# A graph layer on one core: the two kinds of node-sum products regrouped among the five rounds of a period

## The reference

```python
h = jnp.maximum(_layernorm(x, axis=-1), 0.0)
msg = h[src] + edge_attr_64
agg = jax.ops.segment_sum(msg, dst, num_segments=6250)
out = x + (jax.nn.relu(agg @ W1 + b1) @ W2 + b2)      # W1: 64 x 128, W2: 128 x 64
```

## Time and profile before

| | |
|---|---|
| median of 3 runs | 521.0 us (520.02 to 521.77) |
| the profiled execution | 520.01 us, its span 518.3 us |
| PE matmul busy | 460.3 us, 89% of the span |
| DVE busy | 434.3 us, 84% |
| ACT busy | 380.4 us, 73% |
| POOL busy | 317.0 us, 61% |
| granted TensorE clock, mean | 0.988 of full |

### The profile page before, as it was taken

How to read it: one execution, slowest core, us unless ns; L and a number is a source line. 1 busy time by engine, 2 the same in 40 slices (tenths; PEclk the granted TensorE clock), 3 DMA queues, 4 the chain that set the end, 5 groups by cost and what they waited for, 6 DMA issues and landing times.

```text
span 518.3 us, 27579 instructions
## 1 busy us (share of the span) xinstructions
PE 460.3 (89%) x12541; PEld 406.6 (78%) x12541; DVE 434.3 (84%) x531; ACT 380.4 (73%) x481; POOL 317.0 (61%) x223
## 2 busy tenths in 40 slices
PE   1012799999999999999999999999999999999994
PEld 1002688898898889889888988988898888888883
DVE  4989977989988988998898899889889989969550
ACT  2846766877877887788787878878787877878720
POOL 4379999846576576658757666767765665225200
PEclk9999979999999999999999999999999999999997
DMA  9758058743653573465367347436735743651300
GB/s 197 192 143 253 25 141 200 208 119 114 190 168 98 157 207 113 119 193 147 94 181 205 100 131 196 131 104 187 198 86 143 204 123 106 186 170 51 90 3 10
DMA packets 139626, 73.65 MB, mean 142 GB/s; under 512 B 23644, under 2 KB 137550, under 8 KB 139382
## 3 DMA queue, kind: packets, MB, share of 16 engines
q1 hardware_dynamic: 136105, 65.30, 45.7%
q0 software_dynamic: 3168, 4.90, 3.6%
q10 hardware_dynamic: 234, 1.65, 0.9%
HBM read 66.98 MB, written 4.86 MB: 139 GB/s over the span
## 4 chain that ended last, share of the span: by engine, by line
PE 85%; POOL 6%; DMA 3%; ACT 2%; DVE 2%; issue 1%; SPq 0%; ACTq 0%; DVEq 0%; POOLq 0%
PE sum_ps L846 26%; PE sum_ps L868 21%; PE count_ps L833 17%; PE sum_ps L854 14%; POOL ell L511 3%; PE sum_ps L883 3%; PE sum_ps L890 3%; POOL g L491 2%; DMA comb_rows<-counts 1%; PE sum_ps L818 1%; DMA dst_sb<-in_dst 1%; DMA ell<-comb_rows,ell_idx 1%; ACT counts L345 1%; ACT counts L347 1%; POOL r_f L498 1%
## 5 line engine op out<-in xcount | busy, mean ns | idle before, releaser
L409 ACT CAST counts<-count_ps 128x882 bf16<-128x882 f32 (+2 forms) x369 | 327.1, 978 | 59.7 <-PE count_ps L833 58.6
L677 DVE TENSOR_TENSOR lo_hot<-iota_lo,codes 128x3328 bf16<-128x3328 bf16 (+3 forms) x123 | 228.9, 1861 | 43.1 <-PE count_ps L833 26.4
L511 POOL DMA_INDIRECT ell<-comb_rows,ell_idx x50 | 96.6, 1932 | 92.2 <-DVE ell_idx L649 58.8
L846 PE MATMUL sum_ps<-counts,h_parts 128*128 128x256 bf16 (+1 forms) x1225 | 146.1, 273 | 0.0
L846 PEld LDWEIGHTS sum_ps<-counts,h_parts 128*128 128x128 bf16 x1225 | 114.8, 99 | 18.5
L833 PE MATMUL count_ps<-hi_hot,lo_hot 64*128 64x49 bf16 x6256 | 110.5, 183 | 16.5 <-DVE hi_hot L677 14.8
L833 PEld LDWEIGHTS count_ps<-hi_hot,lo_hot 64*128 64x128 bf16 x6256 | 96.1, 94 | 36.9 <-DVE hi_hot L677 18.0
L491 POOL DMA_INDIRECT g<-in_dst,row_i x49 | 95.0, 1938 | 45.0 <-DVE e_hot L691 29.0
L868 PE MATMUL sum_ps<-e_hot,edges 128*64 128x24 f32 x3528 | 113.1, 217 | 0.5 <-issue 0.5
L868 PEld LDWEIGHTS sum_ps<-e_hot,edges 128*64 128x64 f32 x3528 | 107.9, 139 | 3.2 <-issue 0.6
L677 DVE TENSOR_TENSOR hi_hot<-iota_hi,codes 128x1300 bf16<-128x1300 bf16 (+3 forms) x123 | 105.2, 856 | 0.0
(11 more groups left out here) (107 smaller groups left out, 208.9 us busy)
## 6 DMA issues: line engine op xcount, KB each, us to landing
edges<-in_edge_attr SPq DMA_DIRECT2D x98, 576.0 KB, 5.2
h_rows<-h_sb SPq DMA_DIRECT2D x1, 1568.0 KB, 10.6
x_sb<-in_x SPq DMA_DIRECT2D x4, 384.0 KB, 10.4
out<-o_sb SPq DMA_DIRECT2D x24, 64.0 KB, 1.7
comb_rows<-counts ACTq DMA_DIRECT2D x1, 1443.8 KB
dst_rows<-in_dst SPq DMA_DIRECT2D x49, 18.0 KB
ell<-comb_rows,ell_idx POOLq DMA_INDIRECT x50, 4.0
g<-in_dst,row_i POOLq DMA_INDIRECT x49, 3.9
```

The source lines that it names most:

```text
L409: nc.scalar.copy(counts[j % 2][:, :, 0:2 * half].rearrange("p s (h i) -> p h s i", h=2)[:, :, :, first + a:first + b], count_ps[u % 3][:, ...
L511: nc.gpsimd.indirect_dma_start(out=ell[j % 2][0:rows, h, :, :].rearrange("p s w -> p (s w)"), out_offset=None, in_=comb_dram[:, :], in_off ...
L677: return nc.vector.tensor_tensor(out_ap.rearrange("p i (a t) -> p i a t", t=2), bc(table_ap.rearrange("p (o a t) -> p o a t", o=1, t=2), [ ...
L846: nc.tensor.matmul(sum_ps[m % 2][:, 0:cols], parts[:, s, 0:2 * F], counts[m % 2][:, s, 0:cols], start=(s == 0), stop=False, skip_group_che ...
```

## The change

Only the two tables that deal the node-sum products to the rounds are changed. Nothing else is moved on any other engine, no instruction is added or dropped, and none is made larger or smaller.

```diff
-                HIGH = [0, 20, 20, 40, 40, 49]
-                LOW = [0, 0, 5, 5, 17, 49]
+                HIGH = [0, 24, 24, 49, 49, 49]
+                LOW = [0, 0, 0, 0, 0, 49]
```

## The result

The changed kernel takes 532.37 us at the median of 6 runs (531.04 to 533.89), the kernel before 521.08 us (6 runs beside them, 518.56 to 521.77). The ratio is 1.0208, with a 95% interval from 1.0185 to 1.023: about 2% slower. The profiled execution took 531.46 us with a span of 529.9 us; the one before had 518.3 us, so 11.6 us are to be found.

The account below looks back on a forecast made before the run. PE was taken to bound the kernel, with ACT's copies just fitting rounds 3 and 4. 520.0 - 1.0 (start) + 11.3 (middle) - 0.4 (end) = 529.9, plus 1.0 for the median: 530.9 us; own range 528 to 533, whole range 526 to 537.

Parts of the forecast that it names:

- The seams: Between PE's product groups: a change of the array's split costs about 0.10 us; PE alone saves 0.12 us a period.
- The seam that stood in no row: Edge matmuls followed by counting: taken as 2.12 + 0.10 = 2.22 us, with ends 2.12 and 2.30.
- The stall: Last third of round 4's counting: PE waits 0.67 us for ACT's round 3 copy in every period.
- PE alone decides: Rival, 7%: ACT's last round 3 copy ends early enough, no stall comes; 517.1 us.
- partly absorbed: Rival, 4%: part of the stall goes, for instance by faster ACT copies beside fewer products; half gives 524 us.
- The sum of the middle: Fourth to last counting period: 21 x 0.55 = 11.5 us, less 0.2 in period 22, gives +11.3.
- the 0.2 us foreseen for period 22: Period 22: one product more ahead of round 4 fills part of the stall, 0.2 us less.
- The start: Second period: moved products fill PE's idle time for DVE's tables, clock may stay up; -1.0 us, ends -2.3 and 0.
- The clock rival: Rival, 9%: idle time beside edge products lowers the clock, 2.75 us a fall; every third period gives about 550 us.
- DVE: DVE's batches: no cost, spare time of over 1 us a period; its waits for PE up some 12 us.
- the shortest stretch of two rounds: Counting that DVE's batches need two rounds earlier: rounds 3 and 4 named as shortest, 7.47 us against 7.58.
- at most 0.4 us later: End of the edge products that SP's loads of edges wait for; costed at nothing, with four buffers.

Follow-up runs that it names:

- low_kept: Changed kernel with table LOW as in the kernel before (5, 12, 32) and only HIGH changed; 543.31 us, ratio 1.0232.
- twelve_back: Changed kernel with 12 of the 64-column products put back into round 3, HIGH as changed; 556.19 us, ratio 1.0387.
- short_copies: Changed kernel with ACT's three round 3 copies taking only the first tile of each pair in periods 2 to 23; 551.27 us, ratio 1.0421.
- before_here: The kernel before, unchanged, run again on the third chip; 522.05 us, ratio 0.9991.
- changed_here: The changed kernel as it is, run again on the third chip; 532.26 us, ratio 1.0191.
- turns_first: Changed kernel with PE's turns of round 2 ahead of that round's 25 products, from the fourth period on; 549.07 us, ratio 1.0346.
- six_back: Changed kernel with 6 of the 64-column products put back into round 3; 546.56 us, ratio 1.0302.

## Why the prediction was right, point by point

**The seams.** Right. Rounds 0 to 3 were forecast at 4.02, 3.58, 3.73 and 3.20 us and measured 4.02, 3.58, 3.72 and 3.20. The seam that stood in no row, edges followed by counting, cost 259.87 - 257.65 = 2.22 us, the 0.10 that I chose out of 0 to 0.18. Without the stall, `low_kept`, `twelve_back` and `short_copies` show 18.13, 18.14 and 18.11 us a period; the forecast for PE alone was 18.13.

**The stall.** Right in place, cause, number and size. I gave 0.67 us, 21 times, in the last third of round 4's counting. The starts say 0.66 (1.11 - 0.45). The idle time that the profile notes is 0.50, because the end of the matmul before lies over the rest. Period: 18.80 forecast, 18.78 measured. Round 4 with its stall was forecast at 3.60 + 0.67 = 4.27 us and took 4.26. The rival *PE alone decides* is refuted by the changed kernel's own rows, *partly absorbed* too: the copies did not get faster beside fewer products, 3.21 against 3.22 us.

**The sum of the middle.** 11.3 was forecast, 10.24 came. The periods themselves gave 21 x 0.53 = 11.1. The difference lies in what the two executions had besides: the stretch of before held a wait on "issue" of 1.14 us at 101.35, that of after one of 0.78 at 102.55; and before lost 0.4 us in its last full period (466.15 to 484.80). Of the 0.2 us foreseen for period 22 the stall shows it, with a noted wait of 0.27 us, not 0.50, but the 49 products behind it took 3.02 us instead of 2.85: the period is 18.95 us against 18.45 before, 0.50 more. The second pair of profiles confirms the size: from the fourth period's start to the end of the span, 419.7 us in before_here (523.0 - 103.30), 428.9 in changed_here (532.0 - 103.15), so +9.2, against +10.1 in the first pair (428.8 - 418.8) and 10.9 forecast.

**The start.** This is the term that was mis-sized: -1.0 with ends -2.3 and 0, and +1.55 came. The step that failed was to price "In the second period PE idles 0.93 us for DVE's tables ahead of round 3, and the granted clock is at 0.50, 1.2 GHz, in the stretch behind it" as a loss that belongs to the kernel and comes in every execution, and to let the periods behind it stand as they were. The timeline of PE after:

```profile
69.95 0.81 PE L833 MATMUL count_ps<-hi_hot,lo_hot 64*128 64x49 bf16 x50 [0.21 <-DVE hi_hot L677]
...
77.21 0.68 PE L833 MATMUL count_ps<-hi_hot,lo_hot 64*128 64x49 bf16 x40
79.07 0.33 PE L833 MATMUL count_ps<-hi_hot,lo_hot 64*128 64x49 bf16 x12 [1.18 <-issue]
...
87.04 1.35 PE L868 MATMUL sum_ps<-e_hot,edges 128*64 128x24 f32 x40 [1.99 <-issue]
```

The idle time for DVE did shrink, to 0.21, the clock did stay up, and by 77.21 PE had 80.65 - 77.21 = 3.44 us in hand against the earlier trace rows. The third period lost them again, with waits on "issue" of 1.18 and 1.99 us and a fall of the clock to 0.50 (1.2 GHz) from 88.7 to 92.1. But the kernel before does the same in its other profile, before_here: there PE idled 0.92 us for DVE ahead of round 3, the clock stayed at 1.00 all the same, and the loss came in the third period, with 2.71 us of "issue" and then the clock at 0.50. The timeline of PE in before_here, and two stretches of it:

```profile
70.96 0.81 PE L833 MATMUL count_ps<-hi_hot,lo_hot 64*128 64x49 bf16 x50 [0.92 <-DVE hi_hot L677]
...
88.38 2.12 PE L868 MATMUL sum_ps<-e_hot,edges 128*64 128x24 f32 x36 [2.71 <-issue]
...
103.30 0.68 PE L833 MATMUL count_ps<-hi_hot,lo_hot 64*128 64x49 bf16 x39
...
72.20:78.30 6.10, 6.10 (x165) 5.42 (x161) 6.10 (x6) 4.79 (x6) 6.10 (x1) 1.00 0.49 144
88.40:92.40 4.00, 3.73 (x93) 3.28 (x92) 3.98 (x8) 0.49 (x1) 0.41 (x1) 0.50 0.05 13
```

The fourth period of one and the same kernel began at 99.53 and at 103.30 us, that of the changed one at 101.08 and 103.15. Two profiles of each differ by up to 3.8 us in the start, so the start held no term that could be read from one of them, neither -1.0 nor +1.55. The forecast of 530.9 was 1.5 us below the measured median. That it came so near is in part luck: against the profiles the start was forecast 2.55 us too low and the middle 1.06 us too high, which took off part of it.

**The clock rival.** Not seen in the middle: 0.50 us of noted idle time beside the edge products in each period, and a clock of 1.00 from 105 to 496 us.

**DVE.** The effect was nothing, as forecast, but the sign that I named was wrong. DVE's waits for PE did not grow by 12 us: 25.9 us in 40 times against 24.7 in 22. What grew is its wait for ACT's codes, from 15.3 us in 20 times to 29.0; I read it as PE's longer rounds ahead of the turns reaching DVE by way of ACT, but no run takes it apart. Two readings in the prediction were off without effect on the time: by its own lengths the shortest stretch of two rounds is rounds 2 and 3, 7.06 us before and 6.93 after (measured 6.92), not rounds 3 and 4; and the edge products of round 3 begin 12.30 us into the period instead of 11.65, so 0.65 and not at most 0.4 us later.

**A better version.** `low_kept` and `twelve_back` have periods about 0.11 us shorter than the kernel before where nothing disturbs them, 21 x 0.11 = 2.3 us in all. But their measured times were above the kernel before beside them, by 2.3% and 3.9%, with the unexplained waits in them. Neither is shown to beat it, and unmoved they were not run on the third chip. That stays open, and so does why the first two chips gave these waits to kernels that differ by two numbers.

## What to carry to other kernels

Where one engine's last act of a round and another's next start lie 0.06 us apart with no wait noted, the two chains are tied; work may leave the stretch between them only if the other engine's chain gets shorter as well. Compare that chain's length, from where it can first start to where it is needed, with the stretch it must fit into: here that gave a stall of 0.67 us, with no such wait in the middle of the profile before, and 0.66 came. Both the stretch and the chain's start have to be taken from the new order, which `turns_first` missed. And take a second profile of the unchanged kernel before giving a stretch at the start a term of its own.

## What the runs showed of the hardware that was not expected

- Moving PE's program by 128 instructions, with 64 small matmuls in idle time, cost 8% (521.82 to 565.31 us). What is found of it lies in 20 waits of 0.6 to 2.6 us, 36.3 us in all, with a 16 KB packet of the instruction queue 1.2 to 1.5 us ahead of each one's end, and in a clock of 0.96 where it had been 1.00.
- An idle time of 0.92 or 0.93 us ahead of the same matmul was followed by 1.2 GHz in one execution and by 2.4 GHz in another.
- A matmul that waits for an ACT copy started 0.05 to 0.06 us after the copy's end every time it was looked at, in the first period, the changed kernel, `six_back` and `turns_first`.
